# Low-rank products of two FFNs: from fp32 matmuls to high and low fp16 parts

## The reference, cut to what matters

```python
# FFN of layer 0: x is [tokens, 1024], 8 experts of rank 16, top 2 kept
combine = top-2 gates of softmax(x @ W_router.T), renormalised
h   = einsum('nd,erd->ner', x, A_stack) * combine[..., None]        # 128 values a token
out = x @ W_base.T + b_base + einsum('ner,eor->no', h, B_stack) * 2.0
# FFN of layer 1: 4 experts of rank 16, top 2 kept
mid   = einsum('tf,erf->ter', x, A)                                  # 64 values a token
delta = sum over e of gates[e] * einsum('ter,eor->teo', mid, B) * 4.0
```

## Time and profile before

| | us |
|---|---|
| Median of 3 runs (lowest, highest) | 2117.87 (2116.83, 2118.1) |
| The profiled execution, own time | 2117.49 |
| Its span in the trace | 2115.7 |
| PE busy | 1861.9 (88%) |
| DVE busy | 1605.9 (76%) |
| ACT busy | 1267.7 (60%) |
| POOL busy | 1097.1 (52%) |

### The profile page before, as it was taken

How to read it: one execution, slowest core, us unless ns; L and a number is a source line. 1 busy time by engine, 2 the same in 40 slices (tenths; PEclk the granted TensorE clock), 3 DMA queues, 4 the chain that set the end, 5 groups by cost and what they waited for, 6 DMA issues and landing times. The chain is left out here.

```text
span 2115.7 us, 49075 instructions
## 1 busy us (share of the span) xinstructions
PE 1861.9 (88%) x18912; PEld 1131.9 (54%) x18912; DVE 1605.9 (76%) x4622; ACT 1267.7 (60%) x1827; POOL 1097.1 (52%) x902
## 2 busy tenths in 40 slices
PE   5589899999899998989999989999898999998875
PEld 2355555555555555555555555555555555555543
DVE  3677788787888777788877788778778887778853
ACT  4266655666665566665566665566666556666542
POOL 2455554555555465555465555456555545555541
PEclk8899999999999999999999999999999999999985
DMA  5011111111110011110011111001111011111000
GB/s 207 13 38 51 50 37 36 36 40 50 50 50 30 30 50 40 50 50 30 32 47 40 50 50 50 30 30 40 50 50 50 32 36 41 40 50 40 20 1 21
DMA packets 24733, 91.56 MB, mean 43 GB/s; under 512 B 3136, under 2 KB 3264, under 8 KB 24576
## 3 DMA queue, kind: packets, MB, share of 16 engines
q1 hardware_dynamic: 24704, 91.17, 12.2%
HBM read 74.39 MB, written 16.78 MB: 43 GB/s over the span
## 5 line engine op out<-in xcount | busy, mean ns | idle before, releaser
L539 PE MATMUL pb<-w_base_h,even_words 128*128 128x512 f16 x1024 | 324.8, 379 | 0.4 <-ACT mid_t L831 0.4
L1318 POOL TENSOR_TENSOR p_hl<-sc,p_hl 128x512 f16<-128x512 f32 x128 | 177.6, 1387 | 181.7 <-ACT p_hl L720 181.7
L441 PE MATMUL pa<-ctx_a,tab 128*128 128x512 f32 x384 | 203.7, 656 | 34.5 <-ACT q_spec L720 23.3
L820 ACT ACTIVATE q_diag<-sc,par 32x1024 f32<-32x1024 f32 x192 | 215.9, 1141 | 19.9 <-DVE sc L1057 17.5
L441 PE MATMUL pa<-xn_a,tab 128*128 128x512 f32 x384 | 188.9, 615 | 44.0 <-ACT xn_a L720 43.4
L608 PEld LDWEIGHTS pc<-sc_t,v_diag 128*128 128x128 f16 x6144 | 171.3, 97 | 75.8 <-ACT rows_c L720 48.3
L608 PE MATMUL pc<-sc_t,v_diag 128*128 128x32 f16 x6144 | 174.2, 177 | 41.8 <-ACT rows_c L720 41.8
L1361 POOL TENSOR_TENSOR sc<-sc,sc_rec 128x512 f32<-128x512 f32 x128 | 133.9, 1046 | 147.2 <-DVE sc_rec L1133 147.2
L1311 POOL TENSOR_TENSOR rest<-rest,v_im 128x1024 f32<-128x1024 f32 x32 | 75.9, 2371 | 243.7 <-DVE v_im L1018 243.7
L720 ACT ACTIVATE rows_c<-pc 64x256 f32<-64x256 f32 x256 | 96.2, 376 | 165.5 <-PE pc L608 162.3
L539 PE MATMUL pb<-w_base_l,even_words 128*128 128x512 f16 x512 | 193.9, 379 | 0.0
(11 more groups left out here) (142 smaller groups left out, 4998.7 us busy)
## 6 DMA issues: line engine op xcount, KB each, us to landing
x_a<-in_x SPq DMA_DIRECT2D x32, 512.0 KB, 3.3
ctx_a<-in_ctx_in SPq DMA_DIRECT2D x32, 512.0 KB, 3.2
x_res<-in_x SPq DMA_DIRECT2D x32, 512.0 KB, 3.9
ctx_b<-in_ctx_in SPq DMA_DIRECT2D x32, 512.0 KB, 4.1
out<-rows_c SPq DMA_DIRECT2D x32, 512.0 KB, 2.9
v_diag<-in_base_w SPq DMA_DIRECT2D x1, 4096.0 KB, 14.4
tab<-in_spectra SPq DMA_DIRECT2D x1, 576.0 KB, 5.1
q_diag<-in_ra SPq DMA_DIRECT2D x1, 544.0 KB, 15.3
```

Of the source, the lines that this page charges most:

```text
L441: last = mm(place[:, n + h, :], lhsT, moving[:, h * HALF:(h + 1) * HALF], start=True, stop=True)
L539: mm(pb[:, h, :], rows[:, cols], weights[:, j, h * HALF:(h + 1) * HALF], start=(j == 0 and m == 0), stop=False)
L820: nc.scalar.activation(q_diag[rows, :, col:col + QB], source, ACT.Copy, scale=par[rows, a:a + 1]).then_inc(qd_out.sem, 1)
L1318: g_.tensor_tensor(part[:, :, :, LO], sc[:, g % 2, :, :], part[:, :, :, HI], ALU.subtract)\
```

## The change

The gated values get a high and a low fp16 part. `mid` moves from SBUF into free columns of PSUM, and two DVE instructions per FFN write `mid_hl`: the high part as scale times `mid`, rounded to fp16, and the low part as scale times `mid` minus the high part. The FFN's scale moves there from ACT. In layer 0 both parts are transposed one after the other (as fp16) and the product is made of three fp16 products per half of the columns: high by high, high by low, low by high. In layer 1 the 64 high and 64 low columns stand side by side and are transposed as one 128 by 128 block, so that one contraction over 128 rows holds both; it is multiplied by a weight tensor whose both halves hold the high part of B, and by one with the low part of B in the upper half and zeros below. `c_delta` now leaves a result times 256, which `c_result` divides out. The fp32 copies of both B are loaded into unused columns of `q_diag` and split in the setup as the other weights are.

```diff
@@ setup @@
-        CONSTS_SET = 11
-        WEIGHTS_SPLIT = 2
+        CONSTS_SET = 12
+        WEIGHTS_SPLIT = 4
+        mid0_place = pb[:, 0, MID_AT:MID_AT + P].bitcast(F16)
+        mid1_place = pc[:, 0, MID_AT:MID_AT + P // 2].bitcast(F16)
+        mid = [pb[:, 0, 384:384 + P], pc[:, 0, 384:384 + E1 * RANK]]
@@ SP @@
+            sp.dma_start(b0_f32, b0).then_inc(w_in.sem, 16)
+            sp.dma_start(b1_f32[0:E1 * RANK, :], b1).then_inc(w_in.sem, 16)
+            sp.dma_start(b1_f32[E1 * RANK:P, :], b1).then_inc(w_in.sem, 16)
@@ PE @@
             def b_base_end(b):
                 for h in range(2):
-                    last = mm(pb[:, h, :], mid_t[0][:, :], w_b0[:, h * HALF:(h + 1) * HALF],
-                              start=False, stop=True)
+                    cols = slice(h * HALF, (h + 1) * HALF)
+                    mm(pb[:, h, :], mid0_t[:, 0, :], w_b0_h[:, cols], start=False, stop=False)
+                    mm(pb[:, h, :], mid0_t[:, 0, :], w_b0_l[:, cols], start=False, stop=False)
+                    last = mm(pb[:, h, :], mid0_t[:, 1, :], w_b0_h[:, cols], start=False, stop=True)
             def b_mid(b):
-                pe.wait_ge(mid_out[0].sem, mid_out[0].after(b))
-                nc.tensor.transpose(pb[:, 0, MID_AT:MID_AT + P], mid[0][:, :], ident[:, :])\
+                pe.wait_ge(midl_out[0].sem, midl_out[0].after(b))
+                nc.tensor.transpose(mid0_place[:, 0:P], mid_hl[0][:, 0, :], ident_h[:, :])
+                nc.tensor.transpose(mid0_place[:, P:2 * P], mid_hl[0][:, 1, :], ident_h[:, :])\
                     .then_inc(tr_mid[0].sem, 1)
             def c_mid(b):
-                pe.wait_ge(mid_out[1].sem, mid_out[1].after(b))
-                nc.tensor.transpose(pc[:, 0, 384:384 + P], ident[:, :], ident[:, :])
-                nc.tensor.transpose(pc[0:E1 * RANK, 0, MID_AT:MID_AT + P], mid[1][:, :], ident[:, :])\
+                pe.wait_ge(midl_out[1].sem, midl_out[1].after(b))
+                nc.tensor.transpose(mid1_place, mid_hl[1][:, :, :].rearrange("p a r -> p (a r)"), ident_h[:, :])\
                     .then_inc(tr_mid[1].sem, 1)
             def c_delta(b):
-                    last = mm(pc[:, h, :], mid_t[1][:, :], w_b1[:, h * HALF:(h + 1) * HALF],
-                              start=True, stop=True)
+                    cols = slice(h * HALF, (h + 1) * HALF)
+                    mm(pc[:, h, :], mid1_t[:, :], w_b1_hh[:, cols], start=True, stop=False)
+                    last = mm(pc[:, h, :], mid1_t[:, :], w_b1_l0[:, cols], start=False, stop=True)
@@ ACT @@
-                nc.scalar.activation(mid_t[n][:, :], source[0:rows, 0, MID_AT:MID_AT + P], ACT.Copy,
-                                     scale=[SCALE0, SCALE1][n]).then_inc(midt_out[n].sem, 1)
+                if n == 0:
+                    copy(mid0_t[:, :, :].rearrange("p a t -> p (a t)"), mid0_place).then_inc(midt_out[0].sem, 1)
+                else:
+                    copy(mid1_t[:, :], mid1_place).then_inc(midt_out[1].sem, 1)
-            act.wait_ge(w_in.sem, 32)
+            act.wait_ge(w_in.sem, 80)
+            for part, whole in ((w_b0_h, b0_f32), (w_b1_hh, b1_f32)):
+                nc.scalar.activation(part[:, :], whole, ACT.Copy, scale=W_SCALE).then_inc(w_hi.sem, 1)
@@ DVE, after the instruction of L1105 @@
+                dve.wait_ge(mid_out[n].sem, mid_out[n].after(b))
+                v.tensor_scalar(mid_hl[n][:, 0, :], mid[n], unscale, None, ALU.mult)\
+                    .then_inc(midh_out[n].sem, 1)
+                dve.wait_ge(midh_out[n].sem, midh_out[n].after(b))
+                v.scalar_tensor_tensor(out=mid_hl[n][:, 1, :], in0=mid[n], scalar=unscale,
+                                       in1=mid_hl[n][:, 0, :], op0=ALU.mult, op1=ALU.subtract)\
+                    .then_inc(midl_out[n].sem, 1)
@@ DVE @@
-                v.tensor_tensor(rows_c[:, :], pc_all, rows_c[:, :], ALU.add).then_inc(x4_out.sem, 1)
+                v.scalar_tensor_tensor(out=rows_c[:, :], in0=pc_all, scalar=1.0 / W_SCALE, in1=rows_c[:, :],
+                                       op0=ALU.mult, op1=ALU.add).then_inc(x4_out.sem, 1)
@@ DVE, setup @@
+            v.memset(w_b1_l0[E1 * RANK:P, :], 0.0).then_inc(const_set.sem, 1)
+            v.tensor_copy(ident_h[:, :], ident[:, :])
+            v.scalar_tensor_tensor(out=w_b0_l[:, :], in0=b0_f32, scalar=W_SCALE, in1=w_b0_h[:, :],
+                                   op0=ALU.mult, op1=ALU.subtract).then_inc(w_lo.sem, 1)
+            v.scalar_tensor_tensor(out=w_b1_l0[low, :], in0=b1_f32[low, :], scalar=W_SCALE, in1=w_b1_hh[low, :],
+                                   op0=ALU.mult, op1=ALU.subtract).then_inc(w_lo.sem, 1)
```

More of the change, by code:

```diff
@@ L148, in build @@
         w_ra0_l = sb("w_ra0_l", [P, KT, E0 + P], F16)
-        w_b0 = sb("w_b0", [P, D])
+        w_b0_h = sb("w_b0_h", [P, D], F16)
+        w_b0_l = sb("w_b0_l", [P, D], F16)
         w_att = sb("w_att", [P, 4, P])
@@ L152, in build @@
         w_ra1 = sb("w_ra1", [P, KT, E1 + E1 * RANK])
-        w_b1 = sb("w_b1", [E1 * RANK, D])
+        w_b1_hh = sb("w_b1_hh", [P, D], F16)
+        w_b1_l0 = sb("w_b1_l0", [P, D], F16)
         x_a = sb("x_a", [P, D])
@@ L214, in build @@
         gate_rec = [little(1) for n in range(2)]
-        mid = [sb(f"mid{n}", [P, [P, E1 * RANK][n]]) for n in range(2)]
-        mid_t = [sb(f"mid_t{n}", [[P, E1 * RANK][n], P]) for n in range(2)]
+        mid_hl = [sb(f"mid_hl{n}", [P, 2, [P, E1 * RANK][n]], F16) for n in range(2)]
+        mid0_t = sb("mid0_t", [P, 2, P], F16)
+        mid1_t = sb("mid1_t", [P, P], F16)
+        ident_h = sb("ident_h", [P, P], F16)
         bn = [little(2, 6) for n in range(4)]
@@ L306, in build @@
         mid_out = [signal(f"mid_out{n}") for n in range(2)]
+        midh_out = [signal(f"midh_out{n}") for n in range(2)]
+        midl_out = [signal(f"midl_out{n}") for n in range(2)]
         tr_mid = [signal(f"tr_mid{n}") for n in range(2)]
@@ L347, in build @@
         tables = [(tab, spectra), (ident, identity), (band_mask, band), (par, parity)]
-        consts = [(w_b0, b0), (w_att, wqkvo), (bias_att, biases), (w_ra1, ra1), (w_b1, b1)]
+        consts = [(w_att, wqkvo), (bias_att, biases), (w_ra1, ra1)]
         TABLES_IN = 16 * len(tables)
         CONSTS_IN = 16 * (len(consts) + 1)
-        CONSTS_SET = 11
-        WEIGHTS_SPLIT = 2
+        CONSTS_SET = 12
+        WEIGHTS_SPLIT = 4
         base_f32 = v_diag[:, :, :, :].rearrange("p n a c -> p (n a c)")
-        ra0_f32 = q_diag[:, :, :].rearrange("p n c -> p (n c)")[:, 0:KT * (E0 + P)]
+        q_flat = q_diag[:, :, :].rearrange("p n c -> p (n c)")
+        ra0_f32 = q_flat[:, 0:KT * (E0 + P)]
+        b0_f32 = q_flat[:, KT * (E0 + P):KT * (E0 + P) + D]
+        b1_f32 = q_flat[:, KT * (E0 + P) + D:KT * (E0 + P) + 2 * D]
         idle_column = {}
@@ L827, in experts_exp, with experts_mid @@
                                      bias=lg_neg[n][:, :]).then_inc(gt_exp[n].sem, 1)
-            def experts_mid(b, n, source, rows):
+            def experts_mid(b, n):
                 act.wait_ge(tr_mid[n].sem, tr_mid[n].after(b))
-                nc.scalar.activation(mid_t[n][:, :], source[0:rows, 0, MID_AT:MID_AT + P], ACT.Copy,
-                                     scale=[SCALE0, SCALE1][n]).then_inc(midt_out[n].sem, 1)
+                if n == 0:
+                    copy(mid0_t[:, :, :].rearrange("p a t -> p (a t)"), mid0_place).then_inc(midt_out[0].sem, 1)
+                else:
+                    copy(mid1_t[:, :], mid1_place).then_inc(midt_out[1].sem, 1)
             def c_exp(b, g):
@@ L876, in step @@
                     experts_exp(b, 0, pb, E0)
-                    experts_mid(b, 0, pb, P)
+                    experts_mid(b, 0)
                 if do_c:
@@ L919, in step @@
                 if do_c:
-                    experts_mid(c, 1, pc, E1 * RANK)
+                    experts_mid(c, 1)
                 if do_b:
@@ L1104, in gates @@
                 dve.wait_ge(gate_inv[n].sem, gate_inv[n].after(b))
-                v.scalar_tensor_tensor(out=mid[n][:, :].rearrange("p (e r) -> p e r", r=RANK),
+                v.scalar_tensor_tensor(out=mid[n].rearrange("p (e r) -> p e r", r=RANK),
                                        in0=source[:, 0, experts:experts + width].rearrange("p (e r) -> p e r", r=RANK),
@@ L1109, in gates @@
                                        op0=ALU.mult, op1=ALU.mult).then_inc(mid_out[n].sem, 1)
+                unscale = [SCALE0 / W_SCALE, SCALE1][n]
+                dve.wait_ge(mid_out[n].sem, mid_out[n].after(b))
[5 more added lines that the diff above has]
+                    .then_inc(midl_out[n].sem, 1)
             def c_scores(b, g):
@@ L1262, in _ @@
                                        op0=ALU.mult, op1=ALU.subtract).then_inc(w_lo.sem, 1)
+            dve.wait_ge(w_hi.sem, 3)
+            v.scalar_tensor_tensor(out=w_b0_l[:, :], in0=b0_f32, scalar=W_SCALE, in1=w_b0_h[:, :],
+                                   op0=ALU.mult, op1=ALU.subtract).then_inc(w_lo.sem, 1)
```

(4 more changed lines are left out.)

## The result

The changed kernel takes 2124.64 us (median of 7 runs, 2122.91 to 2125.61), the kernel before on the same chips 2116.86 (2115.42 to 2118.1). The ratio is 1.0036, with a 95% interval of 1.0025 to 1.0048: slower by 0.36%, 7.8 us, where 2124.0 was forecast. The profiled execution has a span of 2122.6 against 2115.7, so the two traces account for 6.9 us of it.

What follows compares the result with a forecast made beforehand. Bound taken: ACT and POOL at the step's head, then an ACT-POOL-DVE chain to `c_attend` 2, then packed PE. Middle -0.6, clock +7.6, setup +2.6, end -3.4: +6.2 on 2117.49 gives 2123.7, 2124 as median; range 2108 to 2133.

Steps and rivals of the forecast that it cites:

- Two DVE instructions, 0.63 with waits, arriving as 0.4: Layer 0, middle step: two new DVE instructions delay what follows by 0.63 us; DVE's product starts about 0.4 later.
- POOL is held by DVE's product and carries the shift in full: Middle step: POOL's L1318 waits out DVE's L975, so its end and the chain to `c_attend` 2 come 0.4 us later.
- Rival A: Middle step: DVE's shift does not reach POOL (L975's end moves under 0.2), PE's gain comes through: 2107.5 us; chance 0.20.
- `b_base_end` gains 0.42, so a step without a low stretch changes by -0.02: Layer 0 product on PE: six fp16 records save 0.42 us a step against 0.40 of delay; 30 steps give -0.6 us.
- The clock: 12.5 stretches instead of 8, +7.6: PE behind the longer gap ahead of `c_attend` 2: 4.5 more low-clock stretches at 1.7 us, +7.6 us (0 to +14).
- rival B: Middle steps: chain late as forecast, but PE's clock falls no more often; 2116.5 us, no difference; chance 0.20.
- Layer 1's saving is absorbed ahead of `xn_b`, by 0.9 us of idle time: Head of a middle step: PE saves about 1.0 us in `c_delta`, then waits for POOL before `xn_b`: worth 0.
- Setup +2.6: Program start: DVE's two new subtractions delay POOL and PE by 2.3, identity cast 0.2, step 1 0.1: +2.6 us.
- End -3.4: Last two steps, PE at lower clock: cheaper `c_delta` products save 1.6 and 1.8 us: -3.4 (-2 to -4.5).
- ACT's copy +0.1: Layer 0's ACT copy grows from 128 to 256 columns, 0.1 us longer; POOL is held longer anyway: 0.
- Rival C: New DVE instructions take 0.35 us or more each, +0.23 a step, 15 to 16 clock drops: 2136 us; chance 0.10.

Runs made afterwards that it cites:

- e4: Kernel before plus only layer 0's two DVE instructions, writing a spare tile, with PE's transpose waiting for the second: 2151.44 us, ratio 1.0161 to before.
- e1: Kernel after with DVE's product (a_product) moved ahead of c_sums 2 and c_scores 3: 2082.28 us, ratio 0.9834 to the kernel before.
- e2: Kernel before with DVE's product (a_product) moved ahead of c_sums 2 and c_scores 3: 2096.73 us, ratio 0.991 to the unedited kernel before.
- e9: Kernel before plus layer 0's two DVE instructions alone, and six unused fp16 matmuls ahead of c_attend 2: 2120.83 us, ratio 1.0037 to before.
- e3: Kernel after with six unused fp16 matmuls per full step in PE's wait ahead of c_attend 2: 2112.28 us, ratio 0.9982 to the kernel before.
- e10: Kernel after with three unused fp16 matmuls in PE's wait ahead of c_attend 2: 2111.22 us, ratio 0.9982 to the kernel before.
- e6: Only the layer 1 part of the change, layer 0 as in the kernel before: 2117.13 us, ratio 1.0006 to the kernel before.
- e5: Only the layer 0 part of the change, layer 1's product as in the kernel before: 2124.85 us, ratio 1.0049 to the kernel before.
- e8: Kernel after with DVE's product moved ahead and B's fp32 setup copies moved so POOL waits for two subtractions: 2077.94 us, ratio 0.9826 to before.

## Why the prediction was right

Right in the whole and in its main steps, with several sizes off that partly cancel.

- *Two DVE instructions, 0.63 with waits, arriving as 0.4.* 0.58 with the waits 0.65, arriving as 0.43. Shown to be the cause by e4.
- *POOL is held by DVE's product and carries the shift in full.* 2.07 for 1.75, and the gap of `c_attend` 2 at 1.61 where 1.6 was forecast. The grounds were two durations of one line; e1 and e2 show it. Rival A falls by the same rows: the shift was above its point of decision.
- *`b_base_end` gains 0.42, so a step without a low stretch changes by -0.02.* 62.19 against 62.21; L560's six products begin 0.217 apart. e4, which has the delay and not the gain, gives +0.40 by itself, and e9 the same.
- *The clock: 12.5 stretches instead of 8, +7.6.* 12, and +7.6: four more, and the one before that cost 0.75 instead of 1.7. That they would follow the longer gap held, and e3 and e10 show it by removal, which rules out rival B. The arithmetic (8 times 1.6/1.2) was a guess at a rate, and its second part, one or two left at the old place, was wrong: all 12 are at the new place. Its success is partly luck: the same reasoning for e1, e2 and e4 missed by 7, 4 and 2 to 5 stretches.
- *Layer 1's saving is absorbed ahead of `xn_b`, by 0.9 us of idle time.* Absorbed, yes (e6), but not there: only 0.14 of it is found ahead of `xn_b`'s transposes. PE waits 0.99 instead of 0.79 ahead of `c_delta`, 0.54 for ACT's query blocks ahead of `c_scores` 0, a wait that was not among the rows before, and 0.91 instead of 0.78 ahead of `a_context_long`. The four products take 1.12 to the next one, where under 1.0 was forecast: 0.87 is their issue (four times 0.217), and I have no row for the rest. What I missed is that ACT, which binds the head of the step, does so for the first scores too.
- *Setup +2.6.* The wait of POOL came out at 2.3 as computed. The stretch is 3.2 longer: the product of step 0 is already 0.4 later (16.25 against 15.82), where 0.2 was taken for the cast of the identity. The new setup does begin later (15.91 to 17.98 in its eight traces, 15.20 to 15.82 in the four with the old one), but which of its parts does it isn't shown.
- *End -3.4.* -3.4 by distance; the last `c_delta` 1.93 where 1.9 was forecast. That both products together make the -3.4 isn't shown: e5, without layer 1's new product, ends 2.5 us earlier than the kernel before, and e6, with it alone, 4.0.
- *ACT's copy +0.1.* 384 ns instead of 280, and no effect, since POOL is held longer than that.

Rival C needed 0.35 and more for each new instruction; they took 0.29. Its sum (0.23 more a step and 7 to 8 more low stretches) wasn't far-fetched: in e4 a step is 0.40 longer, and there are 9 more.

Still open: how many stretches fall into a given place. The gaps of 0.40 and 0.78 in the head of the step go with 8 stretches before (7 of them there), 7 in e3, e6 and e10, 3 in e9, 4 in e2, and none in e8, with hardly different gaps. e6 and e8 have the same gaps in the head of a step within 0.02 us (0.96, 0.49, 0.16, 0.26 and 0.96 in e8), yet 7 low stretches and none; what differs is the wait ahead of `c_attend` 2 (1.20 and 0.82) and the length of a step (62.22 and 61.39). Nor do the stretches fall at random: in the kernel after they begin 126.3 or 187.7 us apart, which is every second or third step, in e4 64.9 and 126.3 in turn, in e2 372.1 each time. So a count need not follow from the size of a gap alone, and the length of a step is a rival that no run tests; only the pairs with the same step length (after against e3 and e10, e4 against e9) are free of it. And no run here separates the length of a wait from what PE does around it.

## What to carry to other kernels

Work taken from an engine pays only if the wait that ends last loses it: price first what the change adds on the engine that this wait hangs on, here 0.6 us of DVE instructions ahead of a product that holds up POOL, and ask whether that product can go first (moving it ahead of two others gave 2% in the changed kernel and 0.9% in the kernel before). Where a gap of PE is followed by packed work and the granted clock falls behind it, count those stretches as a cost of the gap of their own (here 1.7 us each behind the long gap), and test it by filling the gap with unused matmuls: if the kernel gets faster, the clock was the loss. A long duration of one instruction that is normal at its next turn points to the instruction beside it.

## What the runs showed of the hardware that I had not expected

- Three unused matmuls in a gap of 1.6 us, 0.97 of it left, removed all 12 stretches of low clock behind it; seven others appeared elsewhere, and the net was 11 us by the ratios and 12.4 by the traces.
- The clock fell by half for 3.4 us (granted 0.50, as the 0.51 of the earlier trace rows; that is 1.2 GHz instead of 2.4) in a kernel in which PE is 86% busy. In the kernel after each time cost 1.7 us; on `a_context_long` it cost 1.7 before and 1.3 in e3, e9 and e10, and one on `a_context` 0.75.
- Between DVE's product and POOL the exclusion, forecast for POOL, is visible in both directions: POOL 1.75 to 2.16 instead of 1.28, DVE 1.48 (mean 1449 ns in e2) instead of 1.22.
